# The key sums of the last attention folded once more on GpSimd, variance offsets moved to GpSimd, and a reordered token choice layer

## What is computed

```python
x = layernorm(x + L0_attn(x))      # attention in a window of 128, 16 heads
x = layernorm(x + L0_ffn(x))       # token choice: 16 tokens a group, 64 experts
x = layernorm(x + L1_attn(x))      # linear attention
x = layernorm(x + L1_ffn(x))       # attention, 8 heads, nested widths
# L0_ffn: every expert takes the token with the greatest logit of its group
logits = einsum('btd,des->btes', grouped, controller) + tie
perm   = (logits == max over t)
sel    = einsum('btd,btes->besd', grouped, perm)
inner  = relu(einsum('besd,desf->besf', sel, f1) + bias)
out    = einsum('besd,btes->btd', einsum('besf,esfd->besd', inner, f2), perm)
# L1_ffn: quarter e of the tokens is cut to its first 256 / 2**e columns
xn = layernorm(x) * norm_w + norm_b
q, k, v = xn[..., :m] @ W[:, :m].T + bias          # all 1024 tokens attend
attn = softmax(q k^T / 16);  out = (attn v) @ o_w[:m, :m].T + o_b + x
```

## Time and profile before

| | |
|---|---|
| time, median of 3 | 2738.49 us (2733.28 to 2750.91) |
| the profiled execution | 2743.36 us, of which the span is 2740.40 us |
| granted clock of PE, mean | 0.93 of 2.4 GHz |
| token choice, nested width attention | 482 us, 794 us of the span |

### The profile page before, as it was taken

One profiled execution on the slowest core, in us unless ns is written; L12 is line 12 of the kernel. 1 busy time (PEld: TensorE's weight loads), 2 busy tenths in 40 slices (PEclk: granted clock), 3 DMA queues, 4 the chain that ended last, 5 costly groups with the idle time before them and its releaser, 6 DMA issues. The chain is left out here.

```text
span 2740.4 us, 43432 instructions
## 1 busy us (share of the span) xinstructions
PE 2242.0 (82%) x17584; PEld 1406.9 (51%) x17584; DVE 1469.8 (54%) x2638; ACT 930.6 (34%) x1337; POOL 905.1 (33%) x509
## 2 busy tenths in 40 slices
PE   2899999999999996787777289988468888988984
PEld 1445555555455554665656145665345555555552
DVE  1445555555555553354545244664466766777672
ACT  0233333333333332543433012222134444443442
POOL 4121211122221200111312143333215664766567
PEclk7899999999999998898989699999689999999997
DMA  6555566555555533556776500110363553445311
GB/s 135 111 109 101 115 114 116 121 101 101 124 111 107 104 68 118 186 191 216 253 247 212 183 31 31 62 42 21 123 161 92 137 149 106 123 116 164 103 47 46
DMA packets 226533, 328.98 MB, mean 120 GB/s; under 512 B 14384, under 2 KB 164128, under 8 KB 226080
## 3 DMA queue, kind: packets, MB, share of 16 engines
q1 hardware_dynamic: 223520, 325.56, 45.2%
q10 hardware_dynamic: 2816, 0.65, 0.2%
HBM read 197.59 MB, written 127.93 MB: 119 GB/s over the span
## 5 line engine op out<-in xcount | busy, mean ns | idle before, releaser
L1574 POOL TENSOR_TENSOR l1f_added<-l1f_probs 128x1024 f32<-128x1024 f32 x120 | 281.4, 2367 | 276.5 <-ACT l1f_probs L1630 276.5
L461 ACT ACTIVATE l0a_probs<-l0a_slot 128x1024 f32<-128x1024 f32 (+1 forms) x256 | 248.4, 971 | 336.0 <-PE l0a_slot L621 188.8
L518 DVE TENSOR_REDUCE l0a_rowmax<-l0a_slot 128x4 f32<-128x1024 f32 (+1 forms) x256 | 293.4, 1156 | 127.6 <-PE l0a_slot L631 124.7
L1630 ACT ACTIVATE l1f_probs<-l1f_slot 128x1024 f32<-128x1024 f32 x240 | 244.6, 1022 | 332.8 <-PE l1f_slot L1805 326.7
L1684 DVE TENSOR_REDUCE l1f_rowmax<-l1f_slot 128x1 f32<-128x1024 f32 x240 | 287.4, 1217 | 59.7 <-PE l1f_slot L1796 59.3
L421 POOL TENSOR_TENSOR l0a_turned<-l0a_turned 128x512 f32<-128x512 f32 x32 | 40.7, 1273 | 557.9 <-DVE l0a_turned L504 557.9
L1805 PE MATMUL l1f_slot<-l1f_Qs,l1f_Ks 128*128 128x256 f32 x960 | 173.8, 305 | 49.7 <-DVE l1f_rowmax L1684 23.4
L1796 PE MATMUL l1f_slot<-l1f_Ks,l1f_Qs 96*128 96x512 f32 x480 | 176.8, 454 | 31.1 <-DVE l1f_rowmax L1684 21.8
L1805 PEld LDWEIGHTS l1f_slot<-l1f_Qs,l1f_Ks 128*128 128x128 f32 x960 | 145.7, 196 | 105.9 <-DVE l1f_rowmax L1684 43.9
L621 PE MATMUL l0a_slot<-l0a_mask,l0a_ident 128*128 128x512 bf16 (+1 forms) x512 | 150.4, 376 | 25.3 <-issue 23.0
L563 PE MATMUL l0a_O<-l0a_probs,l0a_V 128*32 128x128 f32 x3840 | 156.5, 279 | 10.3 <-issue 10.3
(11 more groups left out here) (190 smaller groups left out, 4070.2 us busy)
## 6 DMA issues: line engine op xcount, KB each, us to landing
expert_outputs<-l0f_wide SPq DMA_DIRECT2D x64, 512.0 KB, 3.9
l0f_wide<-expert_outputs SPq DMA_DIRECT2D x32, 1024.0 KB, 9.5
l0a_Qs<-qk_rows SPq DMA_DIRECT2D x96, 256.0 KB, 7.8
l0a_Ks<-qk_rows SPq DMA_DIRECT2D x96, 256.0 KB, 14.8
l1f_Ks<-kq_rows SPq DMA_DIRECT2D x48, 512.0 KB, 8.0
l0f_f<-in_dram SPq DMA_DIRECT2D x10, 2048.0 KB, 15.4
qk_rows<-l0a_hi SPq DMA_DIRECT2D x32, 512.0 KB, 2.8
qk_rows<-l0a_lo SPq DMA_DIRECT2D x32, 512.0 KB, 4.2
```

Source lines behind the costliest of these rows:

```text
L461: exp_ready.by(act.activation(probs[:, t % 2, HG * g:HG * g + HG, 0:reach, :], s[:, :, 0:reach, :], ACT.Exp, scale=SCALE))
L518: max_ready.by(dve.reduce_max(rowmax[:, t, :, 2 * g:2 * g + 2], s[:, :, :, first:2 * P], AX))
L1574: add_done.by(pool.tensor_tensor(added[:, u, :], probs[:, 0, u, :], probs[:, 1, u, :], ALU.add))
L1630: exp_done.by(act.activation(probs[:, half, u - FIRST[b], :], s[:, :], ACT.Exp, scale=SCALE))
```

## The change

1. Nested width attention: after adding the halves POOL adds the upper two of the four key tiles to the lower two (128x512, in place), behind a wait for its own first addition. The sum on PE takes two key tiles in place of four. ACT's wait for free `probs` goes by the first addition (`halved`), PE's by the second (`add_done`).
2. Every layer norm: the offset of the variances is issued by POOL in place of DVE.
3. Token choice: the order of the steps. The first two transposes of a half come before the last experts of the other half, the late outs start one step later, "aggregate" comes behind the first h, "rescale" between the experts, both stores stand ahead of gather 0, and the loads and f2 straight behind it. The early outs come later, and out3 ahead of the logits. The first `lo` of the first block is DVE's, and in the last block DVE rescales 14 of 16 tiles.

```diff
@@ -169,11 +169,11 @@
             dve.bn_aggr(self.mv[:, t, :], self.stats[:, t, :]).then_inc(self.aggregated, 1)
-        dve.wait_ge(self.aggregated, n * self.tiles)
-        dve.tensor_scalar(self.mv[:, :, 1], self.mv[:, :, 1], LN_EPS, None, ALU.add).then_inc(self.var_ready, 1)
...
 
+        pool.wait_ge(self.aggregated, self.count(b, use) * self.tiles)
+        pool.tensor_scalar(self.mv[:, :, 1], self.mv[:, :, 1], LN_EPS, None, ALU.add).then_inc(self.var_ready, 1)
@@ -688,12 +688,15 @@
     s, e, late = selection(0), experts(0), combination(-1, 1)
-    steps = [(-1, "gather", 1), (0, "f2", 0)] + s[:10] + merged(s[10:], late) + [(0, "spread", 1)]
-    steps += e[:4] + [(-1, "aggregate", 0)] + e[4:] + [(0, "gather", 0)]
+    turned = selection(1)[:2]
+    steps = [(-1, "gather", 1), (0, "f2", 0)] + s[2:11] + merged(s[11:], late[:3]) + [late[3], (0, "spread", 1)]
+    steps += e[:1] + [(-1, "aggregate", 0)] + e[1:5] + [(-1, "rescale", 0), e[5], (-1, "rescale", 1), e[6], (-1, "rescale", 2), e[7],
+                                                        (-1, "rescale", 3), turned[0], e[8], turned[1], e[9]]
+    steps += [(-1, "store", 1), (-1, "store", 0), (0, "gather", 0), (1, "load", 0), (1, "load", 1), (0, "f2", 1)]
     s, e, early = selection(1), experts(1), combination(0, 0)
-    steps += merged(s[:10], [(-1, "rescale", n) for n in range(4)] + [(-1, "store", 0), (-1, "store", 1), (1, "load", 0), (1, "load", 1), (0, "f2", 1)])
-    steps += merged(s[10:], early[:2]) + [(1, "xT", 0), (1, "xT", 1), early[2], (1, "xT", 2), (1, "xT", 3), (1, "logits", 0), early[3]]
-    steps += [(1, "spread", 0)] + e[:4] + [(1, "second", 0)] + e[4:6] + [(1, "hi", 0), (1, "lo", 0)] + e[6:8] + [(1, "hi", 1), (1, "lo", 1)] + e[8:]
+    steps += s[2:14] + merged(s[14:], early[:1]) + [early[1], (1, "xT", 0), (1, "xT", 1), early[2], (1, "xT", 2), (1, "xT", 3), early[3]]
+    steps += [(1, "logits", 0), (1, "spread", 0)] + e[:4] + [(1, "second", 0)] + e[4:6] + [(1, "hi", 0), (1, "lo", 0)] + e[6:8]
+    steps += [(1, "hi", 1), (1, "lo", 1), (1, "pT", 0), e[8], (1, "pT", 1), e[9]]
@@ -727,7 +730,7 @@
         xT_even = signal("xT_even", CH); xT_odd = signal("xT_odd", CH)
-        hi_ready = signal("hi_ready", 2); lo_ready = signal("lo_ready", 2)
+        hi_ready = signal("hi_ready", 2); lo_ready = [signal(f"lo_ready{n}", 1) for n in range(2)]
@@ -756,10 +759,15 @@
 
-        def rescale(eng, X, n, tiles):
+        def low(eng, X, n):
+            part = slice(NT * n, NT * n + NT)
+            hi_ready.wait(eng, X, n + 1)
+            lo_ready[n].by(eng.tensor_tensor(lo[:, part, :], x[:, X % 2, part, :], words(hi[:, part, :]), ALU.subtract))
+
+        def rescale(eng, X, tiles):
...
             for t in tiles:
-                normed[n].by(eng.tensor_scalar(x[:, X % 2, t, :], x[:, X % 2, t, :], ln.mv[:, t, 0:1], ln.rstd[:, t:t + 1],
+                normed[t // NT].by(eng.tensor_scalar(x[:, X % 2, t, :], x[:, X % 2, t, :], ln.mv[:, t, 0:1], ln.rstd[:, t:t + 1],
@@ -808,21 +816,20 @@
         def _(pool):
-            for s in (lo_ready, spread_ready[1], normed[0]):
+            for s in (lo_ready[1], spread_ready[1], normed[0]):
...
                 _, kind, i = step
-                if kind == "lo":
-                    part = slice(NT * i, NT * i + NT)
-                    hi_ready.wait(pool, X, i + 1)
-                    lo_ready.by(pool.tensor_tensor(lo[:, part, :], x[:, X % 2, part, :], words(hi[:, part, :]), ALU.subtract))
+                if kind == "lo" and (X or i):
+                    low(pool, X, i)
...
                     alone(pool)
-                    lo_ready.wait(pool, X)
+                    for ready in lo_ready:
+                        ready.wait(pool, X)
@@ -835,7 +842,7 @@
                     ln.reciprocal_root(pool, X, 0)
-                    rescale(pool, X, 0, range(NT))
+                    rescale(pool, X, range(NT) if X + 1 < NB else range(2))
@@ -847,7 +854,7 @@
                 schedule.wait_filled(act, X if i >= 2 else X - 1, ("sel", (i - 2) % (2 * TP)))
-                s = arrived(act, X, (0, "pT", i))[:, 0:2 * P].rearrange("p (t n) -> p t n", t=2)
+                s = arrived(act, X, schedule.by_name["pT", i])[:, 0:2 * P].rearrange("p (t n) -> p t n", t=2)
@@ -896,7 +903,7 @@
         def _(dve):
-            for s in (xT_odd, rated, best_ready, choice_ready, normed[1], sel_odd, hidden_odd, inter_odd, summed):
+            for s in (xT_odd, rated, best_ready, choice_ready, lo_ready[0], normed[1], sel_odd, hidden_odd, inter_odd, summed):
@@ -928,7 +935,9 @@
                 if kind == "rescale":
-                    rescale(dve, X, 1, range(NT + 2 * i, NT + 2 * i + 2))
+                    rescale(dve, X, range(NT + 2 * i, NT + 2 * i + 2) if X + 1 < NB else ((2, 3, 4), (5, 6, 7), (8, 9, 10, 11), (12, 13, 14, 15))[i])
+                if kind == "lo" and X == 0 and i == 0:
+                    low(dve, X, 0)
@@ -951,7 +960,8 @@
                     if i == 0:
-                        lo_ready.wait(dve, X)
+                        for ready in lo_ready:
+                            ready.wait(dve, X)
@@ -987,7 +997,7 @@
                     if i < TP and i % (TP // 2) == 0:
-                        lo_ready.wait(pe, X, 2 * i // TP + 1)
+                        lo_ready[2 * i // TP].wait(pe, X)
@@ -1371,7 +1381,7 @@
     NSTAGE = 2 * NB
-    HKT = NT // 2
+    HKT, SKT = NT // 2, NT // 4
@@ -1459,7 +1469,7 @@
         exp_done = signal("exp_done", 2 * NU); pv_done = signal("pv_done", 2 * NB)
-        add_done = signal("add_done", NU); sum_done = signal("sum_done", NB)
+        halved = signal("halved", NU); add_done = signal("add_done", NU); sum_done = signal("sum_done", NB)
@@ -1540,7 +1550,7 @@
         def _(pool):
-            x2_ready.start(pool); add_done.start(pool)
+            x2_ready.start(pool); halved.start(pool); add_done.start(pool)
@@ -1571,7 +1581,9 @@
                     sum_done.wait(pool, X if b else X - 1, b if b else NB)
-                    add_done.by(pool.tensor_tensor(added[:, u, :], probs[:, 0, u, :], probs[:, 1, u, :], ALU.add))
+                    halved.by(pool.tensor_tensor(added[:, u, :], probs[:, 0, u, :], probs[:, 1, u, :], ALU.add))
+                    halved.wait(pool, X, i + 1)
+                    add_done.by(pool.tensor_tensor(added[:, u, 0:SKT * QW], added[:, u, 0:SKT * QW], added[:, u, SKT * QW:HKT * QW], ALU.add))
@@ -1626,7 +1638,7 @@
                     behind = (FIRST[b - 1] if b else FIRST[NB - 1]) + min(u - FIRST[b] + 1, len(BATCHES[b - 1]))
-                    add_done.wait(act, X if b else X - 1, behind)
+                    halved.wait(act, X if b else X - 1, behind)
@@ -1742,10 +1754,10 @@
                     add_done.wait(pe, X, FIRST[i] + units)
-                    for j in range(HKT):
+                    for j in range(SKT):
...
                             last = mm(OS[i % 2][DH * u:DH * u + DH, 1, :], ones[:, :], added[:, u, QW * j:QW * j + QW],
-                                      start=False, stop=j == HKT - 1, skip_group_check=True, tile_position=(0, DH * u))
+                                      start=False, stop=j == SKT - 1, skip_group_check=True, tile_position=(0, DH * u))
```

## The result

The changed kernel takes 2764.4 us (median of 10 runs, 2755.9 to 2769.1) beside 2743.4 us of the kernel before (10 runs): a ratio of 1.0077, interval 1.0058 to 1.0096. It is 0.8% slower, within the 1% that the prediction called "same"; 2756 was forecast. But the near total hides two misses of opposite sign. From the first DMA of x in each layer to that of the next (or to the end), token choice went from 483.6 to 457.1 us (-26.5, forecast -15) and nested width attention from 794.6 to 842.0 (+47.4, forecast +33). The rest is the first layer (+4.8) and the third (-0.6); the first varies as much between kernels that run the same code there. Token choice varies too: nine kernels, the changed one among them, run the same code there and take 455.5 to 462.0 us, by one trace each.

What follows compares the result with a forecast made beforehand. PE was taken to bound the last layer, with POOL's bunched list setting one stretch after the change. 27 + 6 - 15 = +18 us gave 2761 on the profiled execution, 2756 against the median; range 2724 to 2784.

Steps and rivals of the forecast that it cites:

- forecast -15: Token choice: earlier loads -6, f2 -3, last store -4 and first `lo` -2.1 us, bounds 0 and -30.
- forecast +33: Last layer: +27 us from POOL's later folds and +6 from PE's clock falling after stalls.
- POOL's chain: Last layer, stage 3's first add to the end of the shift: 44.2 us where it was 35.2.
- This stretch grows by 4.7 us: Last layer, stage 3's first add to nat8: later by 4.7 us; less outside sums, each sequence gets 2.9 us longer.
- the clock: +6: Last layer: PE's stall lowers its clock, 1 us in each of six sequences, bounds 0 to 18.
- sum 3: 6 x -0.9 = -5.4: Last layer: a sum outside the stretch, halved to two key tiles, gives PE 0.93 us back per sequence.
- nothing hides this gain by itself, for PE is the busiest engine: Last layer: each halved sum gives 0.93 us back, four in a sequence, since PE is busiest.
- The offset: Offset of the variances moved to POOL: frees about 1.8 us of DVE a sequence, worth nothing in the second to seventh.
- f2 isn't held up: -3: Token choice, last block: f2 no longer waits behind the stores, its 3.0 us wait goes.
- waits that give PE its clock back: Rival: token choice gains twice as much because fewer waits restore PE's clock; 2741 us, 15%.
- the stores might push the gather: Rival: token choice gains nothing because the stores stand ahead of the gather in one queue; 2771 us, 12%.
- POOL's lateness is absorbed: Rival: last layer gains about 20 us instead of losing, with token choice -35; 2703 us, 12%.

Runs made afterwards that it cites:

- x10: Changed kernel with the last four of eight rescale tiles of the last layer on DVE, at rescale steps 2 and 3: 2727.4 us, ratio 0.9933.
- x2: Kernel before with the fold alone (POOL's second addition, sums over two key tiles): 2786.4 us, ratio 1.0156.
- x1: Changed kernel without the fold; PE sums four key tiles, offset and order as changed: 2703.3 us, ratio 0.9848.
- x4: Kernel before with the offset of the variances on POOL alone: 2725.3 us, ratio 0.9939.
- x3: Changed kernel with folds in batches 0 and 3 alone, the other two summed over four key tiles: 2701.0 us, ratio 0.9839.
- x9: Kernel x1 with sums over two of four key tiles, half of the sums left out, so values are wrong: 2685.8 us, ratio 0.9788.
- x11: Changed kernel with the fold in batch 3 alone, sums 0 to 2 over four key tiles: 2707.9 us, ratio 0.9862.
- x7: Changed kernel with six unread 128x512 products on PE before sum 2 in five sequences: 2763.5 us, ratio 1.0069.

## Where the prediction held and where it failed

**POOL's chain held to 0.3 us.** The chain took 43.96 (44.2), nat8 stood at 46.20 (46.3), the fold took 1277 ns at the median (1276), 120 times; POOL's busy time and PE's two waits came as forecast. The walk along POOL's list from rows of before was right, and x10 showed that the chain is the cause, not only that it stands beside it. The walk also said rightly that the gains of sum 1, sum 2 and the offset would vanish inside it; the fold alone costs 40 us of last layer in x2, and 64 in the changed kernel against x1.

**What it was set against failed.** "This stretch grows by 4.7 us" was taken for six sequences from one of them, as if they were alike. But they alternate (the rows under x4). In the kernel before nat8 stands 41.5 or 41.6 us behind the first add in the third and the fifth sequence, but 38.5 in the second, fourth and sixth and 37.3 in the seventh; in the changed kernel it is 46.2, and 43.3 in the seventh. So the stretch grows by 4.6 or 4.7 in two of the six, by 7.7 in three and by 6.0 in one. All six together, from the first sum of the second sequence to that of the eighth, by the timelines of PE and POOL:

| part of a sequence | before, us | changed, us | growth | forecast |
|---|---|---|---|---|
| first add of stage 3 to nat8 | 236.0 | 274.3 | +38.3 | 6 x 4.7 = +28.2 |
| nat8 to sum 3 | 106.4 | 114.1 | +7.7 | the clock: +6 |
| sum 3 to sum 0 | 148.3 | 146.0 | -2.3 | sum 3: 6 x -0.9 = -5.4 |
| sum 0 to the first add | 30.1 | 23.0 | -7.1 | sum 0: -5.4 |
| together | 520.8 | 557.4 | +36.7 | +23.4 |

Of the 13 us that are missing, 10 are the stretch that was taken from one sequence. Sum 3 gave back 0.4 us a sequence and not 0.9 (0.3 in the steady ones, as in x3, x9 and x11): "nothing hides this gain by itself, for PE is the busiest engine" was false there, since busiest in the mean is not the one that every wait ends on. Sum 0 gave more than was asked of it, for it ran at the half clock in two of the six and before in three. The clock was nearly right: +7.7 for 6, and its upper bound of 18 was not reached. The last sequence grew by 13.0 us (11.7), the first got 2 shorter as forecast. The Trainium skill, "TensorE: Matmul & The Clock Gate", section "HAM oscillation", is right that waits between bursts lower the clock again; the trace agrees in all six sequences, but the price is what PE does behind the last wait, not the whole slow time.

**The offset was worth more than it seemed.** I had its gain at 1.8 us of DVE and hidden in all sequences but the first. Hidden is right. Alone it gives 3.3 a sequence (x4), and the granted clock rises from 0.96 to 1.00 with it, for sum 0 no longer runs at the half clock in every second sequence.

**Token choice was undervalued by some 11 us** (7 to 13 by the other traces of the same code). The start gained 3.5 (forecast 2.1), each of the two middle blocks some 4.7 (3, from transposes 3.3 us less late in the rows above), the last block 13.3 (7). The tail at its end came as forecast (39.6 to 35.6, -4.0). Of the 11 more than half are in the last block, and there the step "f2 isn't held up: -3" was too small. Before, PE's timeline has this:

```profile
1494.95 3.50 PE L1039 MATMUL l0f_slot<-l0f_f,l0f_hidden 64*128 64x256 f32 x16 [3.00 <-DMA l0f_f<-in_dram]
```

After, its counterpart:

```profile
1479.31 2.00 PE L1049 MATMUL l0f_slot<-l0f_f,l0f_hidden 64*128 64x256 f32 x16 [0.78 <-DVE l0f_hidden L952]
```

The wait gave 2.2, and the products behind it 1.5 more, at the full clock. Some 5 us more, where the outs and the last gather came sooner, I had at nothing; what brought them is not taken apart here. This is the rival "waits that give PE its clock back", in small. That the stores might push the gather, the rival against it, didn't come: the gather was to run 2 us later, and it went out at 1246.86, 2.1 us sooner than before.

**The rivals.** "POOL's lateness is absorbed" is refuted by ACT's 10.23 us. The forecast total was 8 us low. Five of these come from its base, a median of three runs, 2738.5, where ten runs give 2743.4; only 3 are left because the +14 of the last layer and the -11 of token choice nearly cancelled. The mechanism was the stated one, the closeness of the total was chance.

## What to carry to other kernels

Before giving work to an engine that is a third idle, walk its list from the first instruction of a bunch to the one that another engine waits for; what lies between is the price, whatever the mean says, and the gain on the other side must be looked for at the next wait, not in the busy time. Moving two instructions of 1.1 us off the engine that the bottleneck waits for (x4) gave more than halving the bottleneck's own instructions outside the stall (x3). And before one sequence is taken for all, look at the next one: here every second one was 5 us shorter, and that was most of the error in the last layer. Of three edits in one change try each alone: two of these make the kernel 1.5% faster (x1, 2703 us; with x3's folds in two batches 2701), the third makes the whole slower than before.

## What the hardware showed beyond expectation

- Behind waits of 2.55 us (the changed kernel) and 3.51 us (x7) PE ran at 1.2 GHz for 5.5 us, in x7 although it had been busy up to that wait. Behind one of 0.49 us in x3 the same products run at full clock (0.73 us).
- DVE's 128x8 tensor_scalar took 172 ns in one layer and 1.10 us at the median in the last (the earlier trace rows has the mean). All thirteen that started inside a POOL add of 128x1024 ended 0.02 to 0.04 us behind it. On POOL it takes 0.24 to 0.31 us. Moving it gave 3.3 us a sequence for 2.1 of DVE's busy time.
- 128x256 tensor_scalar of f32: 402 ns at the median on DVE, 1260 on POOL, in the rescale of token choice of the changed kernel.
